# Perceiver layer on one core: order of copies on the sync queue in the query stage

## The reference

```python
x = x + xattn(layernorm(x), ctx_1024)     # x: 32 x 64 x 512, ctx_1024: 32 x 1601 x 512
x = x + attn(layernorm(x))                # 16 heads, causal, over 64 rows of each sequence
x = x + ffn(layernorm(x))                 # two rounds of a mixture of 64 Kronecker experts, top 2

def xattn(input_seq, condition_seq):
    q = input_seq @ Wq.T + bq
    k = condition_seq @ Wk.T + bk
    v = condition_seq @ Wv.T + bv
    return softmax(q @ k.T) @ v           # one head of width 512
```

## Time and profile before

| | us |
|---|---|
| median of 3 runs | 1326.34 |
| lowest and highest | 1323.18, 1327.03 |
| the profiled execution's own time | 1326.24 |
| its span | 1324.2 |

### The profile page before, as it was taken

The page is one execution under the profiler, slowest core; times in us unless marked ns, Lnnn a source line. Parts: engine busy times, 40 slices in busy tenths (PEclk is TensorE's granted clock), DMA queues, the critical chain, the costliest instruction groups (busy, mean ns, idle before and its releaser), DMA issues.

```text
span 1324.2 us, 61286 instructions
## 1 busy us (share of the span) xinstructions
PE 1235.5 (93%) x27823; PEld 799.4 (60%) x27823; DVE 809.8 (61%) x1523; ACT 439.6 (33%) x866; POOL 227.7 (17%) x373
## 2 busy tenths in 40 slices
PE   9999999999999999999999998887889888889885
PEld 6764333333333334677666775666777776779775
DVE  5567767776777671455565555555674846465766
ACT  2223211321132112221222211235464646454564
POOL 1000000000000001121122211115252533212212
PEclk9899999999999999999999999898999998995998
DMA  7976899899989983511001110301321306334002
GB/s 296 319 217 197 311 298 310 273 319 293 314 273 318 293 288 81 90 64 63 32 32 63 63 48 34 95 33 65 127 103 55 127 2 252 150 140 191 31 32 95
DMA packets 68176, 211.50 MB, mean 160 GB/s; under 512 B 14544, under 2 KB 30928, under 8 KB 53616
## 3 DMA queue, kind: packets, MB, share of 16 engines
q1 hardware_dynamic: 68080, 210.16, 47.0%
HBM read 172.37 MB, written 37.75 MB: 159 GB/s over the span
## 4 chain that ended last, share of the span: by engine, by line
PE 77%; DVE 10%; issue 5%; DMA 3%; POOL 2%; ACT 2%; SPq 1%; DVEq 0%; POOLq 0%; ACTq 0%
PE ps L715 14%; PE ps L564 10%; PE ps L1088 8%; PE ps L2192 6%; PE ps L2143 4%; PE ps L235 4%; PE ps L1202 4%; PE ps L1109 4%; DVE arena L576 4%; PE ps L479 3%; PE ps L2121 2%; PE ps L2234 2%; PE ps L705 2%; DVE arena L1872 2%; PE ps L2178 2%
## 5 line engine op out<-in xcount | busy, mean ns | idle before, releaser
L576 DVE STREAM_TRANSPOSE arena<-arena 128x448 f32<-128x448 f32 (+1 forms) x512 | 264.0, 578 | 100.8 <-PE ps L564 83.8
L564 PE MATMUL ps<-arena 32*64 32x400 f32 (+1 forms) x4096 | 202.7, 506 | 0.8
L715 PE MATMUL ps<-arena 128*64 128x512 f32 x832 | 189.1, 598 | 0.0
L564 PEld LDWEIGHTS ps<-arena 32*64 32x64 f32 x4096 | 75.3, 130 | 97.2 <-issue 50.7
L715 PEld LDWEIGHTS ps<-arena 128*64 128x64 f32 x832 | 55.5, 136 | 121.3 <-issue 111.9
L599 ACT ACTIVATE arena<-ps,arena 128x384 f32<-128x384 f32 x64 | 36.3, 582 | 276.4 <-DVE arena L590 276.4
L1088 PE MATMUL ps<-arena 128*128 128x256 f32 x512 | 115.1, 383 | 0.8 <-ACT arena L1023 0.8
L1088 PEld LDWEIGHTS ps<-arena 128*128 128x128 f32 x512 | 97.2, 191 | 17.5 <-issue 3.3
L2042 ACT COPY arena<-ps 128x512 f32<-128x512 f32 x128 | 75.1, 588 | 84.3 <-PE ps L2192 57.8
L1872 DVE SCALAR_TENSOR_TENSOR arena<-ps,arena 128x512 f32<-128x512 f32 x64 | 69.8, 1117 | 38.8 <-PE ps L2178 38.4
L888 POOL TENSOR_TENSOR arena<-arena 128x1024 f32<-128x1024 f32 x8 | 18.9, 2368 | 405.8 <-PE ps L715 405.8
(11 more groups left out here) (158 smaller groups left out, 1824.9 us busy)
## 6 DMA issues: line engine op xcount, KB each, us to landing
arena<-ctx SPq DMA_DIRECT2D x64, 1024.0 KB
arena<-ctx SPq DMA_DIRECT2D x32, 768.0 KB
arena<-q_n SPq DMA_DIRECT2D x64, 256.0 KB, 11.2
h_n<-arena SPq DMA_DIRECT2D x16, 1024.0 KB, 4.4
arena<-h_n SPq DMA_DIRECT2D x16, 1024.0 KB, 10.0
arena<-x SPq DMA_DIRECT2D x16, 512.0 KB, 4.5
arena<-ctx SPq DMA_DIRECT2D x32, 256.0 KB
x_n<-arena SPq DMA_DIRECT2D x16, 512.0 KB, 3.5
```

The costliest lines, as they stand in the source:

```text
L564: last = pe.matmul(ps[b * SEQ:(b + 1) * SEQ, tb, 0:WIDTH[tb]], qs[p % 2][r, db, b * SEQ:(b + 1) * SEQ], z[r, at % RING, b, 0:WIDTH[tb]], s ...
L576: vec.transpose(z[:, at % RING, :, g * 224:g * 224 + nt * 32].rearrange("p b (j t) -> p b j t", t=32), slots[slot_of(k)][:, :, 0:nt, db * ...
L715: last = pe.matmul(ps[b * SEQ:(b + 1) * SEQ, OB, :], probt[:, j, b * SEQ:(b + 1) * SEQ], slot[:, b, jj, :], start=j == 0, stop=j == TILES - 1)
```

## The change

The store of group 1 and the load of row group 5 are issued directly behind the load of row group 4. The first half of context group 2 and the queries of pair 0 follow them, with the second half of context group 2 next. The wait on `s_qd` ahead of the queries is left out; `store_queries(1)`, now ahead of them, has the same wait. No instruction of another engine is changed and no copy is added or taken away.

```diff
@@ -308,11 +308,10 @@
         load_context(sp, a, slots, s_c, 1, (1,))
         store_queries(0)
         load_rows(4)
-        load_context(sp, a, slots, s_c, 2, (0,))
-        sp.wait_ge(s_qd, 8 * 16)
-        load_queries(sp, a, qs, s_qs, 0)
         store_queries(1)
         load_rows(5)
+        load_context(sp, a, slots, s_c, 2, (0,))
+        load_queries(sp, a, qs, s_qs, 0)
         load_context(sp, a, slots, s_c, 2, (1,))
         store_queries(2)
         load_rows(6)
```

## The result

The changed kernel takes 1330.69 us (median of 12 runs, 1326.19 to 1333.23), the kernel before, in as many runs beside it, 1326.24. The ratio is 1.0037, with a 95% interval of 1.0025 to 1.0049: 4.4 us slower by the medians. The ratios in this document leave out runs more than 1.5% above the fastest of their kernel, which are three of nine in e10 and one of twelve in e12. The stall ahead of the transposes of group 5 is gone, and a longer one stands ahead of score 4.

A forecast was written before the change was run, and what follows sets the result against it. The prediction took TensorE's wait for row load 5, and the slow clock after it, as the bound at the edit. Its terms, -5.64 + 5.72 + 2.93 = +3.0 us, gave 1329.3 us from 1326.3, range 1322.0 to 1332.5.

The forecast's parts named there:

- Old stall and its slow clock: TensorE at group 5's transposes: 2.71 us stall plus 2.93 us at half clock, 5.64 us, would go with load 5 earlier.
- Load 6 late by the bytes ahead of it: Row load 6 would land at 65.8, behind pushed-back context halves and queries, though score 4 needed it by 60.1.
- the 18.0 us for 6.29 MB: Time for the queue from load 5 through load 6, taken from the old order's 40 to 58 us at 349 GB/s.
- The later anchor: Second estimate of load 6's landing: 13.1 us between loads 4 and 5, plus one half at 391 GB/s, giving 66.6.
- the slower rival: Deep queue: load 6 lands from 66.8 on, later than its bytes, price past 4 us, +4.7 at 67.5; chance 0.27.
- Stall of 5.72 us: New TensorE stall ahead of score 4, which would wait for block 4 behind late load 6 and start at 72.18.
- Slow clock 2.93 us: TensorE's clock would fall again after the new stall, slowing score 4 and the transposes and products of group 5.
- Store 1 at 205 GB/s: The low queue rate at 46 to 50 us in the kernel before was put down to store 1.
- Queries covered by 2 to 3 us: Queries would land at 56.2 to 57.3, ahead of TensorE's first score, which needs them at 59.40.
- Store 2 issued by 54.8, load 6 near 55: SyncE would issue store 2 from 49.65 to 54.8, then row load 6 at about 55 instead of 58.57.
- The full gain (0.10): Faster rival: load 6 lands by 61.5, stall under 1.5 us; with the clock up, -5.64 to -4.2 us; chance 0.10.
- The clock without a fall (0.08): Rival: TensorE's clock stays at 1.00 through the new stall at score 4, +0.1 us, 1326.4; chance 0.08.

The follow-up runs named there:

- e10: Kernel before, with 12 identity matmuls added behind the first row biases, in its old stall ahead of the transposes of group 5; ratio 1.0088.
- e12: Order of e9, with 4 identity matmuls added ahead of score 4; ratio 0.9974 to the kernel before.
- e1: Changed kernel with the second half of context group 2 moved behind row load 6; ratio 0.9983 to the kernel before.
- e7: Changed kernel with the first half of context group 3 also ahead of store 2 and row load 6; ratio 1.0059 to the kernel before.
- e2: Changed kernel with row load 6 issued ahead of store 2; ratio 1.0026 to the kernel before.
- e3: Changed kernel with 26 identity matmuls, whose results nothing reads, added ahead of score 4; ratio 0.9904 to the kernel before.
- e9: Changed kernel with context group 2's first half back ahead of store 1 and its second half behind row load 6; ratio 0.9984 to the kernel before.
- e4: Changed kernel with both halves of context group 2 moved behind row load 6; ratio 1.0006 to the kernel before.
- e11: Changed kernel with 26 identity matmuls added behind the products of group 7, where there is no stall; ratio 0.9960 to the kernel before.
- e13: Order of e1, with 26 one-column matmuls on a 32 x 32 tile added ahead of score 4; median 1309.16 us, ratio 0.9902 to the kernel before.

## Why the prediction was right or wrong

The forecast was a stall that moves from the transposes of group 5 to score 4, and 1329.3 us with a range of 1322.0 to 1332.5; 1330.69 lies in it. By the steps:

- **Old stall and its slow clock, 5.64 us, gone.** Right. Load 5 landed 7.57 us after load 4 (49.80 - 42.23), forecast 7.51 (48.85 - 41.34).
- **Load 6 late by the bytes ahead of it.** Right in mechanism: e1 (less) and e7 (more) moved it by 5.4 and 3.6 us, and e2 showed that a 7.4 us earlier issue, with the store out of the way, is worth 1.2 us. Its landing came at 66.9 on the clock of before instead of 65.8. The term that was mis-sized is the 18.0 us for 6.29 MB, the old mix's 349 GB/s. From the issue of load 5 to this landing the changed kernel took 21.8 us, so 19.5 less the 2.3 of start and landing, or 323 GB/s; 318 were moved from 46 to 64 us, with 139 in the first two of these, in which the queue was only filling up again. (The window of 40 to 58 us also held store 2 and not load 4, as the prediction lists it; the sum of the bytes is the same.) The later anchor (66.6) was the better one. By my own bound, 66.8, the landing lies at the border between the forecast and the slower rival, and so does the result: 0.37%, with an interval on both sides of 0.3%.
- **Stall of 5.72 us.** Measured 6.61, by that landing. **Slow clock 2.93 us.** Measured 2.63 in the chain, and 2.4 when the stall was filled (e3).
- **Store 1 at 205 GB/s.** Most likely misread: by its place in the queue this rate is the queries', as said above. The sum does not depend on it, since both are among its bytes.
- **Queries covered by 2 to 3 us.** Too much: the copies landed 8.6 to 11.5 us after their issue, and TensorE's weight load for the first scores waited 0.5 us for them. On the path it was about 0.2 us.
- **Sum +3.0.** In the stage it is +3.9, in the whole +4.4. That the sum came so near is no luck of errors that cancel: each of its three terms was met within 1 us.
- **Store 2 issued by 54.8, load 6 near 55.** Wrong: one of the store's copies took SyncE 3.6 us to issue, and load 6 went out at 59.56, 58.7 on the clock of before. It cost next to nothing, since the queue behind was full (e2). I had not listed that ScalarE's results of group 4 wait for store 2, 9.24 us in this trace; that was beside the stall and free.
- **The full gain (0.10).** It asked for load 6 by 60 to 61.5. No order with the same bytes ahead came near. e9, the best, reached 4.2 of the 5.64 us in the stage.
- **The clock without a fall (0.08).** Did not occur at 6.61 us. At 1.47 us (e1), 0.91 (e9) and 0.92 (e10) it did not fall, each time ahead of a score. At 1.35 (e12), with the eight small matmuls of the row biases just ahead, it did, so the length of a stall alone does not tell.

Of the ring order that the Trainium skill states (DMA: Bandwidth & Descriptors, Queues, rings and completion order) e2 is the plainest sign here: 14.4 us from issue to landing with three large steps ahead.

## What to carry to other kernels

On a queue that is full, moving one load up moves every other load down, and the next one in need is the one to price: add up the bytes between its issue and its landing, at the rate that the trace shows for that same mix, and set the landing against its own user's deadline. Look also for how the loads lie among the bulk copies: bulk needed 40 us later belongs between the urgent loads in small portions (e1, e9), neither all ahead (e7) nor all between two of them (e4). When judging a change of few microseconds, compare the stage in the trace as well as the whole time, and not by a single profile; a change in one engine's instruction count can move the end of the program by more than the change itself (here by 14 to 16 us, against 3.9).

## What was not expected

26 added matmuls early in the program shortened the rest by 14 to 16 us (1195.4, 1193.5 and 1194.8 us against 1209.3), wherever they were put and however short they were. All of it lies in the mixture. From the second row biases to its first loop the profiles of before, changed, e3, e11 and e13 take 763.0 to 764.5 us; from there to the last group of matmuls it is 445.6 us before and 444.9 changed, and 432.3, 429.6 and 431.7 in e3, e11 and e13.

4 and 12 added ones did not shorten the profiled execution, and gave spreads of 20 and 27 us between runs. Nor is the number of matmuls the whole story: three runs of e12 were about as quick as e3's, and one of e13's took as long as the kernel before.

What the traces show is that TensorE's idle times without a releaser in the loops of the mixture change place and length, and that the granted clock from 1200 to 1310 us is 1.00 in e11 and 0.87 before. In the kernel before it is 0.50 there for a stretch of some 30 us:

```profile
1190.00:1222.00 32.00, 32.00 (x1275) 30.27 (x1270) 16.94 (x29) 13.85 (x25) 9.98 (x16) 0.50 0.45 170
```

From 320 to 360 us behind the start of that first loop the mean clock is 0.53 to 0.66 in the nine kernels with no added matmul and in e12, and 1.00 in e3, e11 and e13.

That the place of the code sets those idle times, and these the fall of the clock, is a guess that fits this but was not shown: no run moved the code alone, without adding work, and why 26 are good and 12 bad is open. What remains sure is that the time which e3, e11 and e13 save in the mixture is not won by SyncE's order, and that the orders are better compared by the stage than by the whole, within what one profile can tell.
